# The 32-expert stages of a one-core model: token factors by way of memory, gate and up products eight steps ahead

## The reference

```
def _L3_ffn_ref(x, Wg, W1, W2, W3, Ws1, Ws2, Ws3):
    TOP_K = 4
    CAP_FACTOR = 4
    def swiglu(x, w1, w2, w3):
        return jax.nn.silu(x @ w1) * (x @ w3) @ w2
    xf = x.reshape(T, D)                       # T = 2048, D = 128, E = 32
    scores = jax.nn.softmax(xf @ Wg, axis=-1)
    weights, indices = jax.lax.top_k(scores, TOP_K)
    ...
    C = CAP_FACTOR * P // E                    # P = T * TOP_K, C = 1024
    y = jnp.zeros_like(xf)
    for e in range(E):
        ...                                    # the first C tokens that chose e, weights w
        out = swiglu(xg, W1[e], W2[e], W3[e]) * w[:, None]
        y = y.at[tok].add(out)
    z = swiglu(xf, Ws1, Ws2, Ws3)
    return (y + z).reshape(B, S, D)
...
x = x + 0.5 * _L3_ffn_ref(_layernorm(x, axis=-1), ...)
```

## Time and profile before

| | us |
|---|---|
| median of 3 runs | 2299.27 (2298.77 to 2304.78) |
| the profiled execution | 2279.12 |
| its span on the core | 2277.3 |
| stage t1_, norm to loop | about 1349 to 1394.6 |
| stage t2_, norm to loop | 2025.7 to 2070.4 |
| stage t2_, loop | 2070.4 to 2269.5 |

### The profile page before, as it was taken

One profiled execution on the slowest core, in us unless ns is written; L12 is line 12 of the kernel. 1 busy time (PEld: TensorE's weight loads), 2 busy tenths in 40 slices (PEclk: granted clock), 3 DMA queues, 4 the chain that ended last, 5 costly groups with the idle time before them and its releaser, 6 DMA issues. The chain is left out here.

```text
span 2277.3 us, 27349 instructions
## 1 busy us (share of the span) xinstructions
PE 1873.9 (82%) x9342; PEld 997.9 (44%) x9343; DVE 1015.7 (45%) x2387; ACT 777.2 (34%) x1126; POOL 158.9 (7%) x245
## 2 busy tenths in 40 slices
PE   4887996389999889799679988999549982978998
PEld 2334554134333546444344454555423331555554
DVE  2444236577775233410261025444733346674444
ACT  3553231125555323121122112111248853541111
POOL 0001212000000020300110010000200010010000
PEclk9887998679999789899979988999669986689999
DMA  4002110201010211000000000000011001100000
GB/s 157 0 1 115 36 38 27 83 23 43 25 41 2 88 54 36 24 0 0 0 0 0 0 11 7 14 17 10 13 61 40 27 1 47 79 25 7 17 14 29
DMA packets 41139, 69.10 MB, mean 30 GB/s; under 512 B 5204, under 2 KB 33108, under 8 KB 38616
## 3 DMA queue, kind: packets, MB, share of 16 engines
q1 hardware_dynamic: 37840, 57.57, 7.2%
q10 hardware_dynamic: 1159, 6.15, 0.7%
q0 software_dynamic: 2048, 4.20, 0.6%
HBM read 53.09 MB, written 14.61 MB: 30 GB/s over the span
## 5 line engine op out<-in xcount | busy, mean ns | idle before, releaser
L900 PE MATMUL psum<-f_h,w 128*128 128x512 f32 (+1 forms) x512 | 223.4, 594 | 8.6 <-ACT f_h L871 6.2
L1562 DVE TENSOR_REDUCE a_most<-psum 128x1 f32<-128x512 f32 (+3 forms) x304 | 189.6, 660 | 89.3 <-PE psum L1414 75.5
L1534 ACT ACTIVATE a_probs<-psum 128x1024 f32<-128x1024 f32 (+2 forms) x160 | 143.4, 937 | 180.7 <-PE psum L1441 132.2
L2067 ACT ACTIVATE t_silu<-psum 128x512 f32<-128x512 f32 x136 | 81.2, 597 | 344.8 <-PE psum L2133 320.2
L2255 DVE TENSOR_TENSOR t_prod<-t_silu,psum 128x512 f32<-128x512 f32 x128 | 88.0, 688 | 220.3 <-PE psum L2135 220.3
L2144 PEld LDWEIGHTS psum<-t_slot,t_hid 128*128 128x128 f32 x1088 | 145.2, 197 | 54.5 <-issue 34.4
L2144 PE MATMUL psum<-t_slot,t_hid 128*128 128x128 f32 x1088 | 149.2, 282 | 12.2 <-DVE t_hid L2259 7.3
L1411 PE MATMUL psum<-a_ks,a_qs 72*128 72x512 bf16 (+3 forms) x384 | 124.3, 359 | 41.9 <-DMA a_ks<-scratch_k 26.9
L900 PEld LDWEIGHTS psum<-f_h,w 128*128 128x128 f32 x512 | 96.0, 190 | 131.7 <-issue 118.9
L1534 ACT ACTIVATE ga_probs<-psum 128x1024 f32<-128x1024 f32 (+2 forms) x160 | 137.9, 953 | 35.0 <-PE psum L1438 35.0
L2133 PE MATMUL psum<-xnT,t_slot 128*128 128x512 f32 x256 | 133.9, 605 | 15.5 <-PE psum L2144 15.5
(11 more groups left out here) (356 smaller groups left out, 2986.8 us busy)
## 6 DMA issues: line engine op xcount, KB each, us to landing
m_experts<-experts_dram SPq DMA_DIRECT2D x14, 768.0 KB, 10.9
t_slot<-experts_dram SPq DMA_DIRECT2D x34, 192.0 KB, 2.3
a_qs<-scratch_q SPq DMA_DIRECT2D x24, 192.0 KB
a_ks<-scratch_k SPq DMA_DIRECT2D x24, 192.0 KB
ga_qs<-scratch_q SPq DMA_DIRECT2D x24, 192.0 KB
la_qs<-scratch_q SPq DMA_DIRECT2D x24, 192.0 KB
m_rows<-sorted_x SPq DMA_DIRECT2D x46, 64.0 KB, 1.8
w<-w_dram ACTq DMA_DIRECT2D x1, 2888.0 KB, 15.7
```

What stands on the lines that cost most here:

```text
L900: ins = pe.matmul(core.psum[:, HID[n % 2], :], w(name, i * HT + j), src, start=(i == 0), stop=(i == HT - 1))
L1534: act.activation(probs[:, (n * BLOCKS + b) % PROBS, h0:h0 + heads, 0:wide], src, ACT.Exp, scale=SCALE).then_inc(probs_ready, 1)
L1562: v.tensor_reduce(most[:, h0:h0 + heads, at], src, AX.X, ALU.max).then_inc(max_read, 1)
L2067: act.activation(silu[:, buf, :], core.psum[:, bank, :], ACT.Silu).then_inc(silu_ready, 1)
```

## The change

Both calls of `top4_stage` are changed; no other stage is, except that `LayerNorm` can be told its two PSUM banks.

- The factors are no longer split. `factor` is turned in fp32 by four transposes, copied to `turned`, and stored in a DRAM array `factors` of 32 experts x 2048 tokens. For each pair, two loads read one expert's row of 8 KB each and write it to 64 partitions, 512 KB a load, into one of three buffers (`spread`). The products with `select` and the loading of `select` are gone.
- The weights have five slots instead of two.
- TensorE runs gate and up of step n before the down products of step n-8 (`LAG` = 8), with two banks each for gate and up; `prod` has ten buffers. In steps 0 to 11 GpSimd makes `prod`, from a copy of the up product that ScalarE makes (`upper`); these steps are placed among norm, logits and ranks.
- VectorE makes `prod` of step n (`multiply`) and then `hid` of step n-6 (`weigh`), both operands of which are in SBUF.
- The ranks need two VectorE operations instead of three; GpSimd's memsets follow its part of the norm.
- The loops are written out.

```
+    STEPS = NC + PAIRS * NC
+    EARLY = 3 * NC
+    LAG = EARLY - NC
+    SLOTS, FACTORS, PRODS, HIDS = 5, 3, LAG + 2, 2
...
+            for n in range(EARLY):
+                g.wait_ge(silu_ready, n + 1)
+                g.wait_ge(upper_ready, n + 1)
+                if n >= PRODS:
+                    g.wait_ge(down_pe, n - PRODS + 1)
+                g.tensor_tensor(prod[:, n % PRODS, :], silu[:, n % 2, :], upper[:, n % 2, :], ALU.mult).then_inc(early_ready, 1)
...
+            def weights(pair):
+                if pair >= SLOTS:
+                    sp.wait_ge(down_pe, (pair - SLOTS + 2) * NC)
+                sp.dma_start(slot[:, pair % SLOTS, :, :], dram_experts[pair]).then_inc(slot_in[pair % SLOTS], 16)
+
+            def factors(pair):
+                if pair >= FACTORS:
+                    sp.wait_ge(hid_ready, (pair - FACTORS + 1) * NC)
+                for e in range(2):
+                    row = dram_factor[2 * pair + e:2 * pair + e + 1, :].broadcast_to([HALF, N])
+                    sp.dma_start(spread[e * HALF:(e + 1) * HALF, pair % FACTORS, :], row).then_inc(spread_in[pair % FACTORS], 16)
+
+            sp.dma_start(shared[:, :, :], dram_experts[PAIRS]).then_inc(shared_in, 16)
+            for pair in range(SLOTS):
+                weights(pair)
+            sp.wait_ge(turn_copied, 1)
+            for t in range(TPC):
+                rows = dram_factor.rearrange("e (c t q) -> t e c q", t=TPC, q=P)[t]
+                sp.dma_start(rows, turned[t * E:(t + 1) * E, :, :]).then_inc(factor_stored, 16)
+            sp.wait_ge(factor_stored, TPC * 16)
+            for pair in range(PAIRS):
+                factors(pair)
+                if pair + SLOTS < PAIRS:
+                    weights(pair + SLOTS)
...
+            def evacuate(n):
+                act.wait_ge(gate_pe, n + 1)
+                if n >= 2:
+                    prod_done(act, n - 2)
+                act.activation(silu[:, n % 2, :], core.psum[:, g_bank(n), :], ACT.Silu).then_inc(silu_ready, 1)
+                if n < EARLY:
+                    act.wait_ge(up_pe, n + 1)
+                    act.activation(upper[:, n % 2, :], core.psum[:, u_bank(n), :], ACT.Copy).then_inc(upper_ready, 1)
...
-                pe.matmul(core.psum[:, C_BANK, :], select[:, bass.ds(pair * P, P)], parts[:, c * CH:(c + 1) * CH],
-                          start=True, stop=True).then_inc(factor_pe, 1)
...
+            ln.tensor(pe, 0)
+            ln.tensor(pe, 1)
+            logits(0)
+            up(0)
+            ln.tensor(pe, 2)
+            logits(1)
+            up(1)
+            ln.tensor(pe, 3)
+            logits(2)
+            up(2)
+            logits(3)
+            for n in (3, 4, 5):
+                up(n)
+            pe.wait_ge(ln.xnT_ready, NC)
+            down(0)
+            up(6)
             ranks()
+            down(1)
+            for n in (7, 8, 9):
+                up(n)
             turn()
+            up(10)
+            pe.wait_ge(turn_copied, 1)
+            down(2)
+            down(3)
+            up(11)
+            for n in range(EARLY, STEPS):
+                down(n - LAG)
+                up(n)
+            for n in range(STEPS - LAG, STEPS):
+                down(n)
...
+            def weigh(n):
+                pair, c = pair_of(n), n % NC
+                if c == 0:
+                    v.wait_ge(spread_in[pair % FACTORS], 32 * (pair // FACTORS + 1))
+                prod_done(v, n)
+                if n >= NC + HIDS:
+                    v.wait_ge(down_pe, n - HIDS + 1)
+                v.tensor_tensor(hid[:, n % HIDS, :], prod[:, n % PRODS, :], spread[:, pair % FACTORS, c * CH:(c + 1) * CH], ALU.mult).then_inc(hid_ready, 1)
...
+            weigh(NC)
+            weigh(NC + 1)
+            for n in range(EARLY, STEPS):
+                multiply(n)
+                if n + 2 - LAG < STEPS:
+                    weigh(n + 2 - LAG)
```

More of the change, by code:

```diff
@@ L2061, in _ @@
+            ln.scalar(act, 0)
+            ln.scalar(act, 1)
+            for c in range(2, NC):
+                evacuate(c - 2)
                 ln.scalar(act, c)
+            evacuate(2)
             act.wait_ge(shifted, 1)
             act.activation(prob[:, :, :], logit[:, :, :], ACT.Exp).then_inc(exps, 1)
-            def silus(n, buf, bank):
-                act.wait_ge(gate_pe, n + 1)
-                act.activation(silu[:, buf, :], core.psum[:, bank, :], ACT.Silu).then_inc(silu_ready, 1)
@@ L2069, in _ @@
[L2069 to L2080 removed]
+            for n in range(3, EARLY - 2):
+                evacuate(n)
@@ L2082, in _ @@
+            act.wait_ge(turn_pe, 1)
+            act.activation(turned[:, :, :].rearrange("p c q -> p (c q)"), core.psum[:, TURNED, :], ACT.Copy).then_inc(turn_copied, 1)
+            for n in range(EARLY - 2, STEPS):
+                evacuate(n)
         @block.tensor
@@ L2142, in down @@
+            def down(n):
+                c, pair = n % NC, pair_of(n)
+                if pair < 0:
+                    pe.wait_ge(early_ready, n + 1)
+                    left, weights = prod[:, n % PRODS, :], shared[:, 2, :]
+                else:
+                    pe.wait_ge(hid_ready, n - NC + 1)
+                    left, weights = hid[:, n % HIDS, :], slot[:, pair % SLOTS, 2, :]
                 for t in range(TPC):
-                    ins = pe.matmul(core.psum[:, c, t * P:(t + 1) * P], hid[:, buf, t * P:(t + 1) * P], sl[:, 2, :],
-                                    start=first and t == 0, stop=False, skip_group_check=True)
+                    ins = pe.matmul(core.psum[:, c, t * P:(t + 1) * P], left[:, t * P:(t + 1) * P], weights,
+                                    start=pair < 0 and t == 0, stop=False, skip_group_check=True)
@@ L2237, in _ @@
+            v.tensor_tensor(flat(served), flat(served), core.psum[:, RANKS, :], ALU.add).then_inc(ranks_read, 1)
             v.wait_ge(ranks_read, 1)
[L2238 to L2247 removed]
@@ L2261, in _ @@
-            with v.Fori(0, PAIRS // SLOTS) as i:
-                for k in range(STEPS):
-                    multiply(i * STEPS + NC + k, k)
+                if n - PRODS < NC:
+                    v.wait_ge(down_pe, n - PRODS + 1)
+                else:
+                    v.wait_ge(hid_ready, n - PRODS - NC + 1)
+                v.tensor_tensor(prod[:, n % PRODS, :], silu[:, n % 2, :], core.psum[:, u_bank(n), :], ALU.mult).then_inc(prod_ready, 1)
+            weigh(NC)
+            weigh(NC + 1)
@@ L2504, in build @@
         mlp_stage(core, w2, w2_in, "f2_")
-        top4_stage(core, w5, w5_in, masks, select, select_in, dram["experts3"], "t1_")
+        factors = nc.dram_tensor("factors", (32, N), F32, kind="Internal").ap()
+        top4_stage(core, w5, w5_in, dram["experts3"], factors, "t1_")
         norm_stage(core, "n2_")
@@ L2515, in build @@
                     attend_band_stage(core, masks, masks_in, v_all, scratch3, 32, w5_("l_o"), w5_in, core.x, core.xn, "la_")
-        top4_stage(core, w5, w5_in, masks, select, select_in, dram["experts3"], "t2_")
+        top4_stage(core, w5, w5_in, dram["experts3"], factors, "t2_")
         store_stage(core, dram_out, loads)
```

222 lines of the change are left out of this document (74 added, 148 removed).

## The result

The changed kernel takes 2441.68 us (median of four runs, 2424.44 to 2457.4), the kernel before 2301.49 us in the same session (2298.77 to 2304.78): a ratio of 1.061, interval 1.051 to 1.071. The forecast was 2440 us in a range of 2350 to 2530. The four runs of the changed kernel are two at 2424 to 2426 us and two at 2457; the profiled one, 2457.2 us, is of the slower two.

What follows compares the result with a forecast made beforehand. TensorE was taken to pace the loop (187.6 of 199.1 us busy). Terms 9.5 + 2.4 + 153.8 + 104.0 make 269.7 us a stage, 70.6 more; twice, 141, gives 2420 profiled and 2440 us for the runs, range 2350 to 2530.

Steps and rivals of the forecast that it cites:

- TensorE's pace: Routed loop: a step takes 2.62 us without the factor product; 153.8 us a stage against 199.1 if nothing else waited.
- The order on SyncE: SyncE's queue: factors stand behind weights that wait for the previous pair's down products; 11 stalls a stage, 22 in all.
- The wait, 7.9 us: Each stall, from wanting factors to having them: 0.15 + 2.3 + 0.47 + 5.0 us, with ends 5.4 and 16.2.
- The rate of the factor loads: Loads into 64 partitions: 209 GB/s, on a line between 79 and 416, so 5.0 us for 1.05 MB.
- TensorE's idle time: In each stall TensorE is idle for 7.9 + 0.9 - 1.7 = 7.1 us.
- The clock, 2.4 a stall: Idle time in each stall lowers TensorE's clock to 0.50, losing 2.4 us; lower end 0, upper 5 to 8.
- rival 1: Factor loads run at the 128-partition rate: 60 us less, 2380; if the clock also held, 58 less again, 2323; chance 0.20.
- A stalled pair, 19.95 us: Loop: 8.75 of work, 7.9 waiting, 0.9 and 2.4 for the clock, against 10.5 at TensorE's pace.
- The start, 9.5 us later: First routed down products start at 2079.9, where the loop started at 2070.4; early gate and up delay the logits by 7.7.
- the bound of 1.73: Stage start: GpSimd's 512-column product hides beside gate and up if under 1.73 us; at 2.5 it adds 6 a stage.
- The sum: Behind the old loop start a stage takes 9.5 + 2.4 + 153.8 + 104.0 = 269.7 us, 70.6 more; twice, 141.
- From the profiled execution to the median: Whole kernel: 20.2 us added to the profiled execution for the median of the runs; 2420 becomes 2440.

Runs made afterwards that it cites:

- e2: Changed kernel with each pair's weights issued one pair later, so the factors are one pair ahead of them; 2194.61 us, ratio 0.967 to the kernel before.
- e1: Changed kernel with the factors of three pairs ahead issued before the waiting weights on SyncE; 2195.33 us, ratio 0.963 to the kernel before.
- e3: Changed kernel loading only the first half of each factor row and using it twice; 2348.57 us, ratio 1.029 to the kernel before.
- e4: Changed kernel with seven unused fp32 products on TensorE in each stall of pairs 1 to 11; 2357.56 us, ratio 1.036 to the kernel before.
- e8: Changed kernel with each pair's factors replaced by one 128-partition load of different rows from the experts' weights; one run, 2388.08 us.
- e9: Changed kernel with each pair's factors replaced by two 64-partition loads of different rows from the experts' weights; one run, 2447.68 us.
- e7: e2 with GpSimd's twelve products a stage replaced by a memset; one run, 2210.4 us.
- the repeat: The changed kernel measured again, unedited, in a later session; 2426.55 us, ratio 1.067 to the kernel before.
- e10: The kernel of e6 again, five rounds in one session with e11; 2220.69 us, ratio 0.966 to the kernel before.
- e11: The kernel of e2 again, five rounds in one session with e10; 2226.52 us, ratio 0.968 to the kernel before.
- e6: e2 with a lag of twelve steps in place of eight and fourteen buffers for prod; 2203.88 us, ratio 0.967 to the kernel before.
- e5: Changed kernel with the second expert's factor load of each pair issued from ScalarE's queue; 2415.1 us, ratio 1.059 to the kernel before.

## Why the prediction was right, step by step

- **TensorE's pace.** 2.62 a step. e2 shows 10.44 a pair. The last pairs of the changed kernel run so without a gap; one step of them in the chain that ended last:

```profile
2418.83 0.86 PE psum L2162 x2
2419.69 0.86 PE psum L2167 x2
2420.55 0.89 PE psum L2179 x8
```

- **The order on SyncE, eleven stalls a stage.** Right, by the queue's rows and by e1 and e2.
- **The wait, 7.9 us.** 24 waits of VectorE make 204.8 us; less the two at the starts (15.5 and 15.7, which contain time in which VectorE had nothing to do) it is 173.6 / 22 = 7.9. The rate of the factor loads, 5.0 us for a pair's, was the weakest term, interpolated between rows far apart. e3 gives 5.2 (2 x 2.6). That the line came so near was partly luck: its lower end, 79 GB/s, is no rate of a load, since in that stretch of the earlier trace rows the DMA engines were busy for 0.19 of the time only, while SyncE was held 2.15 us by each issue. TensorE's idle time, 7.1 in the forecast, is 6.5 in the stall shown and 8.0 at the longest; without the 7.8 and 7.6 at the two starts it is (166.4 - 15.4) / 22 = 6.9.
- **The clock, 2.4 a stall.** Right, by e4. The reason given, that 7.1 us are more than the 5 after which the clock had fallen in the earlier trace rows, was too narrow: in e3 it falls with 4.2 us of idle time, and in e8 with 4.3. So rival 1's second half, a clock that holds when the stall is shorter, doesn't come: e8, which has rival 1's rate, keeps 2.0 us of the loss a pair. Its first half, 60 us less, is borne out by the waits (61 us less in e8 than in e9). That e8's total is also 60 below e9's is chance, of single runs: its two stages are 83 us shorter, its attention 18 longer.
- **A stalled pair, 19.95 us.** 19.88 in t2_, 20.07 in t1_.
- **The start, 9.5 us later.** The first routed down products start at 2186.47, 53.6 us after the stage's first row, where the loop had started 44.7 after it: 8.9 later. Its terms were off in opposite directions. The logits are 4.8 later and not 7.7. I put the three steps half-way between full and half clock; the first ran at half (2.06 and 1.91 us for its gate and up), the other two at full, and so did the logits of the last two chunks (0.98 us a chunk, in place of 1.75 before), which the sum had left at half clock. From there to the store of the factors it is 21.7 us and not 20.0, and the store takes 4.0 and not 3.3. Of the 1.7, e7 shows 1.4 to be GpSimd's products beside VectorE, which I had counted at nothing as long as a product stayed under 1.73. A product alone takes 1.27, so the bound of 1.73 held, and the cost was on the other engine, where the sum had nothing.
- **The sum.** 70.6 more a stage; measured 75.0 and 70.9, and in the repeat 71.6 and 74.7. In t2_ the part behind the start closes too: from the first routed down products to TensorE's last row it is 261.0 us (2186.47 to 2447.46), where the sum has 2.4 + 153.8 + 104.0 = 260.2. In t1_ it is 263.7; 1.9 of the 3.5 more are its longer stalled pairs.
- **From the profiled execution to the median.** Here the forecast was right partly by luck. The profiled execution was to be 2420 and was 2457, of which 32 us lie outside the two stages, nearly all in the attention at the low clock; the forecast's 20 for the distance to the median came from a profiled execution that was below its median, and this one is above it. The repeat, 2423.1 profiled and 2426.6 in the median, is close to the sum without this term. The differences of the medians, 140 and 155 us, stand on either side of the 141 and 146.

## What to carry to other kernels

On a queue that works in order, a prefetch is only as early as the latest wait ahead of it: three buffers gave no lead here, and one line moved by one turn was worth some 9%. Write down for each load what stands before it and what that waits for, and put what is needed first ahead of what merely has a free slot. Where a stall can't be avoided, its price isn't only its length: the clock took 2.4 us more of each stall of 7 us, and still some 2 us of those of 4.

## What the chip showed that I had not expected

**VectorE and GpSimd.** Where both run a product of two operands from SBUF at the same time, VectorE's 128 x 512 takes 1.60 to 1.64 us instead of 0.69, and GpSimd's three take 4.62 instead of 3 x 1.27. Three of VectorE's and three of GpSimd's take nearly the same 4.9 and 4.6 us; it costs VectorE 0.9 us an operation. GpSimd's memset, which reads nothing, costs it none (0.69 us in e7). The Trainium skill ("SBUF — State Buffer", SBUF: two separate sides) says that VectorE with two operands in SBUF and a GpSimd operation that reads SBUF share a pair of ports under a lock, which one holds for a whole instruction while the other is blocked. The rows agree that each slows the other, but not to the full: strict turns would make 3 x (0.69 + 1.27) = 5.9 us of the six operations, and they take 5.2 (1997.39 to 2002.56).

**The clock in untouched stages.** The attention stages between t1_ and t2_ have two long spells at clock 0.50: 54.6 and 78.5 us before, 92.2 and 133.1 in the changed kernel, 51.2 and 133.1 in its repeat, 41.0 and 78.5 in e1. The work is the same in all. e10, e11 and e6, which have no stalls in the loop, have the long second spell or one in between (133.1, 102.4, 133.1), and so it comes without them. Whether the stalls make it likelier stays open: in all six profiles with a falling clock in the stalls (changed, repeat, e3, e5, e8, e9) the second spell is 109 us or more (in e9 in two pieces), in the other eight it is 72 to 133, and under 80 in four of them (before, e1, e2, e4). Single profiles can't settle it, and the first result's 32 us outside the two stages are therefore not shown to be chance. The spells make 20 to 30 us of a run, more than many changes. What decides them no run here tells.
